# Scatter that adds weighted expert rows to the residual rows, gathers three tiles ahead, one-hot products in four parts, weight pieces in the first 48 steps

## What is computed

```
x = layernorm(x + attention(x))
h = x + causal_attention(rmsnorm(x, g1))
n = rmsnorm(h, g2)
logits = n @ w_router                     # 8 experts
topw, topi = top_k(softmax(logits), 2); topw = topw / sum(topw)
expert_x(n) = (silu(n @ wg[x]) * (n @ wu[x])) @ wd[x]      # 256 -> 704 -> 256
out = layernorm(h + sum over the token's two experts of topw * expert(n))
```

## Time and profile before

| | us |
|---|---|
| median of 3 runs (1528.12 to 1532.54) | 1528.28 |
| the profiled execution | 1529.67 |
| its span | 1527.9 |

### The profile page before, as it was taken

One profiled execution on the slowest core, in us unless ns is written; L12 is line 12 of the kernel. 1 busy time (PEld: TensorE's weight loads), 2 busy tenths in 40 slices (PEclk: granted clock), 3 DMA queues, 4 the chain that ended last, 5 costly groups with the idle time before them and its releaser, 6 DMA issues. The chain is left out here.

```text
span 1527.9 us, 33404 instructions
## 1 busy us (share of the span) xinstructions
PE 1283.7 (84%) x11533; PEld 710.7 (47%) x11534; DVE 968.6 (63%) x1778; ACT 829.9 (54%) x1669; POOL 698.7 (46%) x717
## 2 busy tenths in 40 slices
PE   1799999999999999999999831499999999999910
PEld 0222232223223444444443311388888888888810
DVE  6478888888897888787877317443444434444446
ACT  3148888888878777666666620143443334443313
POOL 2324374546455756666564442524443344433312
PEclk9779999999999999999998865599999999999965
DMA  4417576766675878678666438292111111111136
GB/s 122 83 40 169 160 171 177 193 172 180 178 183 170 232 219 222 198 186 225 205 176 163 147 123 238 54 324 70 45 45 45 41 43 46 45 45 41 39 119 222
DMA packets 162442, 212.23 MB, mean 139 GB/s; under 512 B 28576, under 2 KB 124320, under 8 KB 162336
## 3 DMA queue, kind: packets, MB, share of 16 engines
q1 hardware_dynamic: 154848, 190.38, 45.2%
q0 software_dynamic: 7488, 20.46, 4.4%
HBM read 119.55 MB, written 82.58 MB: 132 GB/s over the span
## 5 line engine op out<-in xcount | busy, mean ns | idle before, releaser
L982 ACT ACTIVATE a_probs<-a_ps_s 128x512 f32<-128x512 f32 (+2 forms) x896 | 460.1, 569 | 172.6 <-PE a_ps_s L777 167.3
L1051 DVE TENSOR_REDUCE a_shift_max<-a_ps_m 128x1 f16<-128x512 f32 x512 | 320.7, 684 | 71.0 <-PE a_ps_m L782 69.7
L782 PE MATMUL a_ps_m<-a_qkx 48*128 48x128 f16 (+3 forms) x1408 | 287.0, 304 | 16.9 <-DVE a_shift_max L1051 8.4
L1568 PE MATMUL e_ps_gu<-e_xT,w_up 128*128 128x256 f16 x2574 | 298.1, 274 | 1.5 <-ACT e_xT L1623 1.4
L777 PE MATMUL a_ps_s<-a_qkx 49*128 49x128 f16 (+3 forms) x1408 | 277.9, 298 | 16.5 <-ACT a_probs L982 14.9
L1568 PEld LDWEIGHTS e_ps_gu<-e_xT,w_up 128*128 x2574 | 249.6, 98 | 35.0 <-issue 5.4
L878 PE MATMUL a_ps_o<-a_probs,a_v_one 128*32 128x512 f32 (+3 forms) x2048 | 237.2, 537 | 2.8 <-ACT a_o L989 2.7
L777 PEld LDWEIGHTS a_ps_s<-a_qkx 49*128 49x128 f16 x1408 | 90.7, 95 | 272.8 <-ACT a_probs L982 156.4
L1530 POOL DMA_INDIRECT y<-e_y,e_put x78 | 77.1, 988 | 250.0 <-DVE e_y L1657 238.1
L1668 DVE TENSOR_TENSOR e_h<-e_gate,e_ps_gu 128x512 f32<-128x512 f32 (+2 forms) x156 | 82.7, 551 | 136.8 <-ACT e_gate L1631 119.0
L1590 PE MATMUL e_ps_y<-w_down,e_h 128*128 x1404 | 162.7, 273 | 7.7 <-issue 5.2
(11 more groups left out here) (191 smaller groups left out, 1617.8 us busy)
## 6 DMA issues: line engine op xcount, KB each, us to landing
a_qkx<-a_qk_dram SPq DMA_DIRECT2D x192, 128.0 KB, 4.3
a_qk_dram<-a_qk SPq DMA_DIRECT2D x32, 512.0 KB, 5.5
a_o_dram<-a_o SPq DMA_DIRECT2D x64, 256.0 KB, 2.7
a_o_half<-a_o_dram SPq DMA_DIRECT2D x32, 256.0 KB
a_inv_half<-a_inv_dram SPq DMA_DIRECT2D x32, 256.0 KB
part<-a_part SPq DMA_DIRECT2D x16, 512.0 KB, 5.7
a_q_swap<-a_q SPq DMA_DIRECT2D x64, 128.0 KB, 3.9
c_rows<-y SPq DMA_DIRECT2D x16, 512.0 KB, 5.4
```

Of the source, the lines that this page charges most:

```text
L782: return pe.matmul(out, qx[first:first + 48, r, pair, q * P:(q + 1) * P], kx[first:first + 48, r, pair, k0:k1], start=start, stop=stop)
L982: act.activation(dst, src, ACT.Exp).then_inc(exp_out, 1)
L1051: vector.tensor_reduce(out, src, AX.X, ALU.max, negate=True).then_inc(max_out, 1)
L1568: mm = pe.matmul(ps_gu[:, bank, kind, f % 2], w[:, ds(e, 1)].rearrange("p o f -> p (o f)"), xT[:, s, xh, k, :], start=n == 0, stop=n == 5)
```

## The change

1. `weights_at(n)` gives piece n to step n for n = 0 to 47, and none to later steps.
2. Routing makes the one-hot tables and products in four parts of 16 columns; DVE makes `by_tile` instead of POOL; ACT writes `by_row` into a tensor of its own; PE interleaves the two sums, in two PSUM banks. SP stores the two shares of each token to memory between the loads of expert 0 and expert 1. DVE makes two further lists: the row of `h` to which a place belongs, and where its share lies.
3. In the expert stage POOL gathers each place's share (`load_share`), DVE scales the result by it, and the scatter adds to the rows of `h` in memory. It waits for the scatter of the tile before. The first 256 rows of the lengthened `h` take the places without a token; SP fills them at the end of attention. POOL's loop is written out, and gathers run three tiles ahead. All of `h` is no longer loaded.
4. The last stage loads `h`, eight batch rows into eight buffers with no wait between, in runs of 4 KB per partition, and has only statistics and normalisation left.

```diff
     def weights_at(n):
-        return [3 * (n // G) + n % G - 1] if group(n) and n % G > 0 else []
+        return [n] if 0 <= n < NW else []
...
-                    dst = x1_dram if plain(u) else t.h_dram
+                    dst = x1_dram if plain(u) else t.h_dram[REST:]
                     sync.dma_start(tiles(dst, u % B), x_res[:, u % 2]).then_inc(x_stored[u % 2], 16)
+                    if u == NU - 1:
+                        rest = t.h_dram[0:REST].rearrange("(k p) n -> p k n", p=P)
+                        sync.dma_start(rest, x_res[:, u % 2, 0:REST // P]).then_inc(rest_filled, 16)
...
-            pool.wait_ge(hot_hi_done, 1)
-            pool.tensor_tensor(by_tile[:], hot_hi[:], tile_no[:].broadcast_to([P, 2 * NT, HI]),
-                               ALU.mult).then_inc(by_tile_done, 1)
...
-            load_experts(sync, t, range(E // 2))
+            load_experts(sync, t, range(1))
+            sync.wait_ge(weighted, 1)
+            sync.dma_start(t.weight_dram.rearrange("(p c k) o -> p (c k o)", p=P, c=2),
+                           t.weight[:].rearrange("p c k -> p (c k)")).then_inc(t.weight_stored, 16)
+            load_experts(sync, t, range(1, E // 2))
...
+            for c in range(PARTS):
+                act.wait_ge(hot_hi_done, c + 1)
+                act.activation(flat(by_row[:, part(c)]), flat(hot_hi[:, part(c)]), ACT.Copy,
+                               scale=row_no[:, 0:1]).then_inc(by_row_done, 1)
...
+            for c in range(PARTS):
+                m = part(c)
+                n = m.stop - m.start
+                vector.tensor_tensor(hot_hi[:, m], hi[:, m].broadcast_to([P, n, HI]),
+                                     count_hi[:].broadcast_to([P, n, HI]), ALU.is_equal).then_inc(hot_hi_done, 1)
+                vector.tensor_tensor(hot_lo[:, m], lo[:, m].broadcast_to([P, n, P]),
+                                     count_lo[:].broadcast_to([P, n, P]), ALU.is_equal).then_inc(hot_done, 1)
+                vector.wait_ge(hot_hi_done, c + 1)
+                vector.tensor_tensor(by_tile[:, m], hot_hi[:, m], tile_no[:, m].broadcast_to([P, n, HI]),
+                                     ALU.mult).then_inc(by_tile_done, 1)
...
                 pool.wait_ge(y_out[s], copied)
+                pool.wait_ge(stored[1 - s], counted(pool, (r + s) * 32))
                 for half in range(2):
-                    pool.indirect_dma_start(t.y_dram, bass.IndirectOffsetOnAxis(ap=put[:, s, half:half + 1], axis=0),
-                                            y[:, s, half], None).then_inc(stored[s], 16)
+                    pool.indirect_dma_start(t.h_dram, bass.IndirectOffsetOnAxis(ap=put[:, s, half:half + 1], axis=0),
+                                            y[:, s, half], None, compute_op=ALU.add).then_inc(stored[s], 16)
+            def load_share(r, s):
...
+                pool.wait_ge(y_out[s], r)
+                for half in range(2):
+                    pool.indirect_dma_start(share[:, s, half:half + 1], None, t.weight_dram,
+                                            bass.IndirectOffsetOnAxis(ap=find[:, s, half:half + 1], axis=0)
+                                            ).then_inc(share_loaded[s], 16)
...
+            gather(1, 0)
+            for m in range(MT):
+                if m + 3 < MT:
+                    gather((m + 3) // 2, (m + 3) % 2)
+                scatter(m // 2, m % 2)
+                if m + 2 < MT:
+                    load_share((m + 2) // 2, m % 2)
...
-                vector.tensor_copy(y[:, s], ps_y[:, s]).then_inc(y_out[s], 1)
+                vector.wait_ge(share_loaded[s], r * 32 + 32)
+                for half in range(2):
+                    op = vector.tensor_scalar(y[:, s, half], ps_y[:, s, half], share[:, s, half:half + 1], None, ALU.mult)
+                op.then_inc(y_out[s], 1)
...
+        rows = lambda x, b: x[b * S:(b + 1) * S].rearrange("(p q) n -> p q n", q=QT)
...
+            for b in range(B):
+                sync.dma_start(z[:, b], rows(t.h_dram[REST:], b)).then_inc(loaded[b], 16)
+            for b in range(B):
+                sync.wait_ge(done, QT * (b + 1))
+                sync.dma_start(rows(out, b), res[:, b]).then_inc(stored, 16)
```

More of the change, by code:

```diff
@@ L30 @@
 HI = SPARE // P
+REST = SLOT
 WP = E * D * F // P // B
@@ L1362, in _ @@
                       skip_group_check=True).then_inc(totalled, 1)
-            pe.wait_ge(hot_done, 1)
-            pe.wait_ge(by_tile_done, 1)
-            for v, values in enumerate((by_tile, by_row)):
-                if v == 1:
-                    pe.wait_ge(by_row_done, 1)
-                for n in range(2 * NT):
-                    mm = pe.matmul(ps_i[0:HI, v], values[:, n, :], hot_lo[:, n, :], start=n == 0,
-                                   stop=n == 2 * NT - 1, skip_group_check=True)
+            for c in range(PARTS):
+                pe.wait_ge(hot_done, c + 1)
+                for v, (values, made_part) in enumerate(((by_row, by_row_done), (by_tile, by_tile_done))):
+                    pe.wait_ge(made_part, c + 1)
+                    for n in range(part(c).start, part(c).stop):
+                        mm = pe.matmul(ps_i[0:HI, v, 0:P], values[:, n, :], hot_lo[:, n, :], start=n == 0,
+                                       stop=n == 2 * NT - 1, skip_group_check=True)
             mm.then_inc(inverse_mm, 1)
@@ L1527, in scatter @@
                 pool.wait_ge(placed[s], copied)
                 pool.wait_ge(y_out[s], copied)
+                pool.wait_ge(stored[1 - s], counted(pool, (r + s) * 32))
                 for half in range(2):
-                    pool.indirect_dma_start(t.y_dram, bass.IndirectOffsetOnAxis(ap=put[:, s, half:half + 1], axis=0),
-                                            y[:, s, half], None).then_inc(stored[s], 16)
-            for s in range(2):
-                gather(0, s)
-            with pool.Fori(0, LAST) as r:
-                for s in range(2):
-                    gather(r + 1, s)
-                    scatter(r, s)
@@ L1542, in _ @@
+            for m in range(2):
+                gather(0, m)
+            pool.wait_ge(t.weight_stored, 16)
+            for m in range(2):
+                load_share(0, m)
+            gather(1, 0)
[5 more added lines that the diff above has]
+                    load_share((m + 2) // 2, m % 2)
             for s in range(2):
@@ L1702, in combine @@
+        stats, mean_var = sb("stats", [P, B, QT, 6], F32), sb("mean_var", [P, B, QT, 2], F32)
+        small = sb("small", [P, B, 4, QT], F32)
         constants = sb("constants", [P, 3, QT], F32)
-        loaded, stored = pair("loaded"), pair("stored")
-        first, summed, stat_out, aggregated, power, mid_out, rstd_out, shift_out, done = map(sem, (
-            "first", "summed", "stat_out", "aggregated", "power", "mid_out", "rstd_out", "shift_out", "done"))
+        loaded = [sem(f"loaded{b}") for b in range(B)]
@@ L1706, in combine @@
+        stored, stat_out, aggregated, power, mid_out, rstd_out, shift_out, done = map(sem, (
+            "stored", "stat_out", "aggregated", "power", "mid_out", "rstd_out", "shift_out", "done"))
         block = ctx.enter_context(nc.Block())
[L1707 to L1708 removed]
+        rows = lambda x, b: x[b * S:(b + 1) * S].rearrange("(p q) n -> p q n", q=QT)
         @block.sync
         def _(sync):
[L1712 to L1724 removed]
+            for b in range(B):
[3 more added lines that the diff above has]
+                sync.dma_start(rows(out, b), res[:, b]).then_inc(stored, 16)
+            sync.wait_ge(stored, 16 * B)
@@ L1765, in weigh @@
+            for b in range(B):
+                vector.wait_ge(loaded[b], 16)
+                for q in range(QT):
+                    vector.bn_stats(stats[:, b, q], z[:, b, q]).then_inc(stat_out, 1)
+                vector.wait_ge(stat_out, QT * (b + 1))
                 for q in range(QT):
-                    vector.bn_aggr(mean_var[:, s, q], stats[:, s, q]).then_inc(aggregated, 1)
-            pipeline(vector, weigh, idle)
+                    vector.bn_aggr(mean_var[:, b, q], stats[:, b, q]).then_inc(aggregated, 1)
```

138 lines of the change are left out of this document (54 added, 84 removed).

## The result

The changed kernel takes 1478.39 us (median of 4 runs, 1474.87 to 1483.32) against 1528.20 (4 runs, 1525.23 to 1532.54) on the same chip: a ratio of 0.9675, 95% interval 0.9647 to 0.9702. The forecast was 1472, its range 1457 to 1489. The profiled execution took 1479.55 us with a span of 1477.6, so the two spans differ by 50.3 us.

| stage | before | after | difference | forecast |
|---|---|---|---|---|
| up to the start of routing | 928.0 | 914.7 | -13.3 | -20 |
| routing | 52.3 | 43.0 | -9.3 | -9.9 |
| experts | 488.8 | 492.1 | +3.3 | +1.6 |
| last stage | 58.7 | 27.8 | -30.9 | -28.0 |

What follows compares the result with a forecast made beforehand. PE was taken to bound the expert stage, DVE to lead in routing and the last stage; attention -20, routing -9.9, experts +1.6 and last stage -28.0 sum to -56.3, giving 1472 us, 8-in-10 range 1457 to 1489.

Steps and rivals of the forecast that it cites:

- the part on the weight pieces: Causal attention, steps 48 to 59: no piece ahead of L603 on POOL gives 4.0 us for two rows, 2.3 for the third.
- 16.3 forecast: Attention steps 48 to 63: 10.3 us gained in the rows at steps 48 to 59 and 6 in the last row.
- The charge of 1.1 us for extra pieces: Attention steps 0 to 47: twelve more pieces cost only 1.1 us for SP's and DMA queues, POOL's idle time covering the rest.
- The drain: End of attention: denominators' load no longer stands behind a weight piece's store in SP's queue, 4.8 us sooner.
- rival A: Attention: another wait takes L603's place, gain there only 0 to -8 us, kernel 1487 us; chance 0.14.
- Routing: Routing stage: tables in quarters with by_tile on DVE, 5.0 us per quarter, PE ends sooner; -9.9 us, bounds -6 and -12.5.
- Experts: Expert stage: rate per tile stays, only the last scatter is on the path; +1.6 us in all.
- Rival B: Expert loop: POOL becomes the bound through dearer adding-scatter issues, kernel slower, 1613 us with issues four times as dear; chance 0.04.
- 2.2 us per tile to spare: Expert loop: of POOL's 5.42 us idle wait per tile, the added copy and two indirect DMAs take 3.2.
- share group: Expert loop: POOL's added copy and two indirect DMA issues for gathering shares, forecast at 3.2 us per tile.
- C: Expert loop: adding scatter lands later than 8.5 us, each tile waits for the one before, 1719 us at 15; chance 0.03.
- The last stage: Last stage: all loads at once, ACT slowest at 2.2 us per row, starting 8.8 us in; 30.7 instead of 58.7, -28.0 us.

Runs made afterwards that it cites:

- pieces in 0, 2 and 3: Kernel before, still three weight pieces in every four of all 64 steps, but in steps 0, 2 and 3 instead of 1, 2 and 3; 1529.22 us against 1527.92.
- the new rule alone: Kernel before with only the new rule for weight pieces, one in each of steps 0 to 47; 1515.21 us against 1527.92, ratio 0.9897.
- plain scatter: Changed kernel with scatters that overwrite the rows of h instead of adding to them; 1478.66 us.
- shares twice: Changed kernel with each share gathered a second time into an unread tensor, two more indirect DMAs per tile on POOL; 1560.51 us, ratio 1.0196 to before.
- no piece in 0: Changed kernel with 36 pieces in the plain steps, 12 in steps 32 to 47 (none where n is a multiple of four), none later; 1484.02 us, ratio 0.9718.
- runs of 1 KB: Changed kernel, its last stage loading and storing rows of 1 KB per partition instead of runs of 4 KB; 1477.39 us, one run.

## Why the prediction was right, and where not

**The sum was right within 7 us, with one step false and some terms mis-sized.** The step that failed is the first of the part on the weight pieces: that the 4.0 us per causal row at steps 48 to 59 come from the piece ahead of L603 on POOL. That rested on a comparison of 46.8 with 50.8 us and on a wait with a named releaser. With that piece moved from step 1 of four to step 0 and the others kept, the wait went and the time did not; of DVE's 21.3 us at L603 PE had felt 4.9. What gives the time is that the steps hold no piece: less POOL work (77.7 instead of 102.4 us in steps 48 to 63), 150 instead of 178 GB/s of transfers, and PE idle 7.6 instead of 16.9 us, at a granted clock of 0.97 instead of 0.91. All eleven kernels without pieces there take 171 to 176 us, the three traces with 12 pieces 187 to 190. POOL's work, its transfers and the clock were not separated further. That the size came out near the forecast is luck, since up to half of it is the clock, which the sum did not have: 17.7 us between the marks in the two first traces, 15.4 by the means of the two traces of before (188.5) and of the five kernels with the new attention (173.1), against 16.3 forecast.

**The charge of 1.1 us for extra pieces** was mis-sized. In the plain steps it is nothing. Steps 32 to 47 lose 7.3 us (198.2 against 191.4 by those means, 6.8). The cover named for it, POOL's 233.6 us of waiting at L547, is mostly in the plain half: of it 20.2 us lie in steps 32 to 47. Why they lose it stays open: it is not the number of pieces (12 in the kernels with pieces in 0, 2 and 3 and with none in 0, as before), not their place alone, not the order of SP's queue. Pieces in all of 32 to 63 in the order of the kernel before give 190.5 and 192.2, no pieces at all 189.3 and 191.3, and every other rule tried 196.7 or more.

**The drain.** The load of the denominators now follows the store of o by 3.0 us (876.65 and 879.68) instead of 7.5, as forecast, but the time from the last mark to routing fell by 1.8 us in the first pair and by 2.4 by the means (40.5 to 38.1), half of the 4.8. The loads did come sooner. PE's wait for the last aT is 4.4 us shorter, but in this trace the work behind it is slower. Before (timeline of PE):

```profile
908.37 2.71 PE L709 MATMUL a_ps_x<-w_proj,a_aT 128*128 128x256 f16 x12 [18.77 <-POOL a_aT L553]
...
911.88 1.48 PE L709 MATMUL a_ps_x<-w_proj,a_aT 128*128 128x256 f16 x12 [0.79 <-DVE a_hid L1141]
```

and in the changed kernel:

```profile
892.86 2.72 PE L714 MATMUL a_ps_x<-w_proj,a_aT 128*128 128x256 f16 x12 [14.36 <-POOL a_aT L558]
...
896.36 2.74 PE L714 MATMUL a_ps_x<-w_proj,a_aT 128*128 128x256 f16 x12 [0.79 <-DVE a_hid L1146]
```

The second product and those behind it ran at the higher clock before and at the lower one here (PE busy 12.7 instead of 10.2 us from the last mark to routing): 2.5 us. In four kernels with no piece after step 47 (the new rule alone, plain scatter, shares twice, no piece in 0) they ran at the higher clock, and the last column is 36.5 to 37.0 us, 3.4 to 4.0 less than before; a fifth, with runs of 1 KB, waited 17.4 us for the last aT and has 39.7. So the term was right for the wait and left out the clock. Attention in all: -13.3 instead of -20. This is rival A in part: some of the gain was given back, though in other steps than it said.

**Routing** -9.3 for -9.9: a quarter took 4.94 us for 5.0.

**Experts** +3.3 for +1.6. The first trace of before was quick here: the three other traces with the old loop have 490.7 to 490.9, the eight with the changed loop 491.0 to 492.9 (492.4 in the mean), so the difference is nearer to 1.6. The last scatter cost 2.2 us (from the start of the last y to the next stage 12.4 for 10.2) instead of 1.5. The rate held: 11.99 us per tile for 11.96 (tiles 11 to 35).

**Rival B was much nearer than the 0.04 it was given.** The forecast had 2.2 us per tile to spare for POOL. Three terms were mis-sized. The 5.42 us idle hold the 0.77 us between a copy and its issue, which are never free; over the loop POOL was idle 5.4 and 6.0 us in turn, so 4.9 in the mean could be used. The share group costs 3.9 us, not 3.2: 3.5 beside plain scatters, as its copy and issue hold that gap too, and 0.4 more because its copy takes 0.77 us behind an adding issue and 0.20 behind a plain one. And the adding issue, 1.60 us instead of 0.99, adds 0.6 once per tile; the second one's excess lies under that copy. So 4.5 us are used, which leaves 0.4, as the kernel with the shares twice shows. C did not come: plain scatters in their place gave nothing.

**The last stage** -30.9 for -28.0. The model held (ACT sets it); a row takes ACT 1.98 us, not 2.2, and it started 8.0 us in, not 8.8. The 4 KB runs were without effect on the stage.

## What to carry to other kernels

A wait that ends with one releaser is not the price of that releaser: move it away alone, and see whether the time goes with it, before the gain is booked. Look first at how much of such a wait the limiting engine felt: here 4.9 of 21.3 us. When an engine off the path takes on work, count the copies and issue gaps around each indirect transfer, take the fixed gap out of what looks idle, and test the margin by doubling the new work; here the sum's margin of 2.2 us was 0.4. Where PE is busy over 90% of the time, compare its busy time for the same instructions as well as its waits: half of a gain may be clock, as here 8.5 of 17.7 us.

## What was not expected of the hardware

- An indirect DMA that adds takes POOL 1.60 us to issue, a plain one of the same shape 0.99, and the DMA engines' busy share for the same bytes is 0.28 instead of 0.15.
- DVE multiplies a 128x4992 bf16 table by a broadcast bf16 column in 5.35 us. POOL took 17.08 with a float32 column, and beside it a DVE sum of 0.47 us took 8.82, so this is not POOL's rate alone.
- POOL's copy of an index takes 0.20 us, but 0.77 right behind an adding issue, and 0.77 us pass from the copy to the first issue even without a wait.
- 512 KB transfers in runs of 1 KB move 348 to 358 GB/s, in runs of 4 KB 387 GB/s, both beside ACT, DVE and POOL at work.
- The same PE instructions (1933 to 1936 in the traces) were busy 173.5 and 170.3 us in two traces of one kernel, at a granted clock of 0.91 and 0.94, and 165.1 us at 0.97 in the changed one.
